# Units of 16 batches in pairs through TensorE, with K and Q products in three rotating PSUM banks

## The chip, the core and the metric

The kernel runs on one core of one Trainium2 chip. The metric is the device time of one execution in microseconds. The core has a tensor engine (PE; its weight loads are recorded apart, as PEld), a vector engine (DVE), a scalar engine (ACT), GpSimd (POOL, not used here) and SyncE (SP), whose queue issues all DMAs. PE writes only to PSUM, which has eight banks of 512 fp32 values per partition.

## The reference

```python
# F: (2048, 64, 128), W: (64, 64, 128), K_w and Q_w: (128, 128), all fp32
Kf = jnp.einsum('bjd,ed->bje', F, K_w)
S = jnp.einsum('bid,bjd->bij', F, Kf)
out = jnp.einsum('bij,ijd->bid', S, W)
out = out + jnp.einsum('bid,ed->bie', F, Q_w)
```

For each of 2048 batches: a projection of 64 tokens by K, the 64 x 64 scores of the tokens with it, then for each row i a product of the scores of all batches with W[i], and a second projection by Q that is added.

## The kernel before

The order on every engine is written out by hand, with semaphores. 2048 batches are 16 tiles (`TILES`) of 128; a tile is 8 units (`UNITS`) of 16 batches, 1024 tokens each, so that there are 128 units. In one step for unit `u` of tile `t`, PE does three blocks in this order:

- `scores(t, u)`: 16 fp32 matmuls with 64 stationary and 64 moving columns, `s_ps<-f_ring,kf`. Two batches alternate between the lower and the upper half of the output partitions. The stationary operand is `kf`, which ACT has copied out of PSUM.
- `rows_out(t - 1, u)`: 8 fp32 matmuls with a contraction over 64 partitions and 128 columns, `o_ps<-s_t,w_sb`, for four rows i of the tile before. They alternate between the lower and the upper half of the input partitions.
- `project(t, u + 1)`: 12 matmuls of 128 x 128 by 512 columns, for the next unit. Each of K and Q takes two banks, and each bank three matmuls: the fp32 product is split into `hi` and `lo` parts (`f_hi`, `f_lo`, `k_hi`, `k_lo`, `q_hi`, `q_lo`).

An fp32 matmul of the first two kinds stands as two records in the trace; so a block of scores has 32 records and a block of rows 16. The PSUM tensors `kf_ps`, `q_ps`, `s_ps` and `o_ps` have two banks each.

ACT does in each step `split_f` (`f_hi` of the unit after next), `copy_kf` (one copy of 1024 elements per partition) and `copy_q` (two of 512). DVE does `copy_s` (three copies of the scores to `s_t`), `sum_out` (`o_ps` + `q_out` to `o_sb`) and its half of the split (`f_lo`). SP issues a load of 512 KB and a store of 512 KB per unit; `o_sb` has two slots, and `sum_out` waits until the store of two units ago has landed. Tile 0 has no rows, and after the last tile 8 blocks of rows alone are left (`body(TILES, 0)`).

Of the kernel before, what the change touches and what calls it, by code (L numbers as in the profile page):

```python
# [5 lines left out]
F32 = mybir.dt.float32  # L6
# [9 lines left out]
UNITS = 8  # L16
UB = P // UNITS
# [3 lines left out]
IR = N // 2 // UNITS  # L21
HALF = N // 2
BANK = 512
RING = 4
# [3 lines left out]
def build(nc, f_t, k_t, q_t, w, out):  # L28
    with ExitStack() as ctx:
# [10 lines left out]
        f_ring = sbuf("f_ring", [D, RING, KP, 2, N])  # L40
        f_hi = sbuf("f_hi", [D, 2, TOK], F32R)
        f_lo = sbuf("f_lo", [D, 2, TOK], F32R)
        kf = sbuf("kf", [D, 2, KP, 2, N])

# [3 lines left out]
        q_out = sbuf("q_out", [D, 2, 2, HALF, P])  # L48
# [8 lines left out]
        kf_ps = psum("kf_ps", [D, 2, BANK])  # L57
        q_ps = psum("q_ps", [D, KP, 2, N])
        s_ps = psum("s_ps", [P, 2, BANK])
        o_ps = psum("o_ps", [D, 2, IR, P])  # L60

        f_in = [sem(f"f_in{n}") for n in range(RING)]
# [4 lines left out]
        qhi_done, qlo_done = sem("qhi_done"), sem("qlo_done")  # L67
        fhi_done, flo_done = sem("fhi_done"), sem("flo_done")
# [22 lines left out]
        def front(t, u):  # L91

            return not isinstance(t, int) or t * UNITS + u < FRONT

# [3 lines left out]
        def _(sp):  # L98
            def load_f(g, slot):
                sp.dma_start(f_ring[:, slot, :, :, :].rearrange("d k h i -> d (k h i)"),  # L100
                             f_t[bass.ds(g, 1), :, :].rearrange("o d n -> (o d) n")
                             ).then_inc(f_in[slot], 16)

            def load_w(half):
                rows = w.rearrange("(m s) j d -> s j m d", s=2)
                sp.dma_start(w_sb[half * N:(half + 1) * N, :, :],
                             rows[half:half + 1, :, :, :].rearrange("o j m d -> (o j) m d")
                             ).then_inc(w_in, 16)
# [8 lines left out]
            load_f(0, 0)  # L117
            sp.dma_start(k_raw[:, :], k_t).then_inc(k_in, 16)
            load_f(1, 1)
            sp.dma_start(q_raw[:, :], q_t).then_inc(q_in, 16)  # L120
            load_f(2, 2)

            def body(t, parity):
                base = t * UNITS
                for u in range(UNITS):
                    if front(t, u + 3):
                        wait(sp, s_done, base + u)
                        load_f(base + (u + 3), (u + 3) % RING)
                    if first(t) and u < 2:
                        load_w(u)  # L130
                    if not first(t):
                        if u > 0:
                            store(t - 1, u - 1, base + (u - 1 - UNITS))
                        elif not (isinstance(t, int) and t == 1):
                            store(t - 2, UNITS - 1, base - (UNITS + 1))
# [7 lines left out]
        def _(act):  # L143
            def split_f(t, u):

                g = t * UNITS + u
                act.wait_ge(f_in[u % RING], t * (UNITS // RING * 16) + (u // RING * 16 + 16))
                wait(act, q_done, g - 1)
                nc.scalar.activation(f_hi[:, u % 2, :],  # L149
                                     f_ring[:, u % RING, :, :, :].rearrange("d k h i -> d (k h i)"),  # L150
                                     COPY).then_inc(fhi_done, 1)

            def copy_kf(t, u):
                g = t * UNITS + u
# [6 lines left out]
            def copy_q(t, u, parity):  # L161
                act.wait_ge(q_done, t * UNITS + u + 1)
                if u == 0:
                    wait(act, out_done, t * UNITS - UNITS)
                src = q_ps[:, :, :, :].rearrange("d k h (m s) -> d s m h k", s=2)
                for s in range(2):
                    rows = src[:, s, :, :, :]
                    if s == 1:
                        rows = rows[:, :, ::-1, :]
# [191 lines left out]
```

## Time and profile before

| | |
|---|---|
| median of three runs | 694.48 us (694.47 to 695.4) |
| the profiled execution | 694.19 us, of which the span of the trace is 692.4 us |
| PE | 666.3 us busy, 96% of the span |
| DVE | 464.9 us, 67% |
| ACT | 393.2 us, 57% |
| q1, all loads and stores | 57.5% of 16 DMA engines, 136.46 MB |

Busy time is the union of an engine's records. A matmul's record starts when it does but its end is modelled, so that neighbours overlap; how far apart two starts are says what a matmul costs in a stream. An entry in square brackets behind a row is the idle time ahead of it and what ended it.

### The profile page before, as it was taken

What the parts mean: (1) busy time and instruction counts of PE and PEld (TensorE: products, weight loads), DVE (VectorE), ACT (ScalarE), POOL (GpSimd) and SP (SyncE); (2) the same over time, 40 slices, a digit from 0 to 9 for tenths busy, and PEclk for the clock granted to TensorE, in tenths of its full rate; (3) what the DMA queues carried; (4) which work ended last, traced back from release to release, by engine and by line L of the source; (5) the groups of instructions that cost most, each with busy time, mean ns of one, the idle gap of its engine ahead of it and who ended that gap; (6) DMA issues with size and microseconds to landing.
All of it is one profiled execution on the core that took longest, in us unless ns stands there. A gap on an engine that the chain in (4) does not pass through costs nothing.

```text
span 692.4 us, 18553 instructions
## 1 busy us (share of the span) xinstructions
PE 666.3 (96%) x7680; PEld 539.0 (78%) x7680; DVE 464.9 (67%) x642; ACT 393.2 (57%) x515; POOL 0.2 (0%) x4
## 2 busy tenths in 40 slices
PE   5999999999999999999999999999999999999953
PEld 4788887887888888878888888788788887888843
DVE  3667677676776776776767767767667677677542
ACT  5775655656656556566566565565665655655500
POOL 0000000000000000000000000000000000000000
PEclk9999999999999999999999999999999999999965
DMA  9645655565565555555555555566556555655333
GB/s 234 176 154 207 213 198 201 212 207 199 203 210 207 194 205 212 204 197 205 212 200 197 209 211 196 199 211 206 198 203 211 206 195 207 213 197 201 124 149 126
DMA packets 57694, 136.90 MB, mean 198 GB/s; under 512 B 4160, under 2 KB 8512, under 8 KB 57664
## 3 DMA queue, kind: packets, MB, share of 16 engines
q1 hardware_dynamic: 57664, 136.46, 57.5%
q8 instruction: 23, 0.38, 0.2%
q14 instruction: 7, 0.06, 0.0%
HBM read 69.34 MB, written 67.11 MB: 197 GB/s over the span
## 4 chain that ended last, share of the span: by engine, by line
PE 96%; DVE 2%; DMA 0%; issue 0%; ACT 0%; SPq 0%
PE o_ps L310 21%; PE s_ps L296 20%; PE kf_ps L272 12%; PE kf_ps L274 9%; PE q_ps L282 9%; PE kf_ps L273 9%; PE q_ps L284 9%; PE q_ps L283 8%; DVE o_sb L235 2%; DMA k_raw<-k_t 0%; DVE f_lo L202 0%; ACT f_hi L149 0%; DVE s_t L221 0%; SPq L100 0%; ACT k_hi L176 0%
## 5 line engine op out<-in xcount | busy, mean ns | idle before, releaser
L157 ACT ACTIVATE kf<-kf_ps 128x1024 f32<-128x1024 f32 x128 | 131.6, 1028 | 213.0 <-PE kf_ps L274 213.0
L218 DVE COPY s_t<-s_ps 128x256 f32<-128x256 f32 x128 | 54.4, 425 | 190.6 <-PE s_ps L296 190.6
L235 DVE TENSOR_TENSOR o_sb<-o_ps,q_out 128x1024 f32<-128x1024 f32 x128 | 156.9, 1225 | 20.6 <-PE o_ps L310 16.9
L310 PE MATMUL o_ps<-s_t,w_sb 64*128 64x128 f32 x2048 | 154.8, 293 | 11.7 <-DVE o_sb L235 11.3
L170 ACT ACTIVATE q_out<-q_ps 128x512 f32<-128x512 f32 x256 | 138.9, 595 | 46.4 <-PE q_ps L284 46.4
L296 PEld LDWEIGHTS s_ps<-f_ring,kf 128*64 128x64 f32 x4096 | 129.8, 138 | 45.1 <-ACT kf L157 44.4
L202 DVE TENSOR_TENSOR f_lo<-f_ring,f_hi 128x1024 fp32r<-128x1024 f32 x128 | 155.5, 1215 | 1.3 <-ACT f_hi L149 1.3
L296 PE MATMUL s_ps<-f_ring,kf 128*64 128x64 f32 x4096 | 147.5, 225 | 0.0
L310 PEld LDWEIGHTS o_ps<-s_t,w_sb 64*128 64x128 f32 x2048 | 129.6, 194 | 22.0 <-DVE o_sb L235 11.6
L149 ACT ACTIVATE f_hi<-f_ring 128x1024 fp32r<-128x1024 f32 x128 | 135.5, 1058 | 0.0
L272 PE MATMUL kf_ps<-f_hi,k_hi 128*128 128x512 f32 x256 | 114.9, 449 | 7.0 <-DVE f_lo L202 7.0
L274 PE MATMUL kf_ps<-f_hi,k_lo 128*128 128x512 f32 x256 | 101.6, 397 | 0.0
L282 PE MATMUL q_ps<-f_hi,q_hi 128*128 128x512 f32 x256 | 101.3, 396 | 0.0
L273 PE MATMUL kf_ps<-f_lo,k_hi 128*128 128x512 f32 x256 | 100.7, 394 | 0.0
L284 PE MATMUL q_ps<-f_hi,q_lo 128*128 128x512 f32 x256 | 100.4, 392 | 0.0
L283 PE MATMUL q_ps<-f_lo,q_hi 128*128 128x512 f32 x256 | 99.8, 390 | 0.0
L272 PEld LDWEIGHTS kf_ps<-f_hi,k_hi 128*128 128x128 f32 x256 | 48.0, 187 | 28.0 <-issue 7.0
L284 PEld LDWEIGHTS q_ps<-f_hi,q_lo 128*128 128x128 f32 x256 | 48.2, 188 | 11.7
L274 PEld LDWEIGHTS kf_ps<-f_hi,k_lo 128*128 128x128 f32 x256 | 48.3, 189 | 11.4
L283 PEld LDWEIGHTS q_ps<-f_lo,q_hi 128*128 128x128 f32 x256 | 48.3, 189 | 11.2
L282 PEld LDWEIGHTS q_ps<-f_hi,q_hi 128*128 128x128 f32 x256 | 48.3, 189 | 10.2
L224 DVE COPY s_t<-s_ps 64x256 f32<-64x256 f32 x128 | 54.6, 427 | 1.7
(11 smaller groups left out, 104.9 us busy)
## 6 DMA issues: line engine op xcount, KB each, us to landing
f_ring<-f_t SPq DMA_DIRECT2D x128, 512.0 KB, 3.3
out<-o_sb SPq DMA_DIRECT2D x128, 512.0 KB, 3.1
w_sb<-w SPq DMA_DIRECT2D x2, 1024.0 KB, 11.6
k_raw<-k_t SPq DMA_DIRECT2D x1, 64.0 KB, 3.1
q_raw<-q_t SPq DMA_DIRECT2D x1, 64.0 KB, 5.2
```

Of the source, the lines that this page charges most:

```text
L149: nc.scalar.activation(f_hi[:, u % 2, :], f_ring[:, u % RING, :, :, :].rearrange("d k h i -> d (k h i)"), COPY).then_inc(fhi_done, 1)
L170: ins = nc.scalar.activation(q_out[:, parity, s, :, u * UB:(u + 1) * UB].rearrange("d m (h k) -> d m h k", h=2), rows, COPY)
L202: nc.vector.tensor_tensor(f_lo[:, u % 2, :], f_ring[:, u % RING, :, :, :].rearrange("d k h i -> d (k h i)"), f_hi[:, u % 2, :].bitcast(F32 ...
L235: nc.vector.tensor_tensor(o_sb[:, slot, :, :], o_ps[:, :, :, :].rearrange("d s m n -> d s (m n)"), q_out[:, parity, :, u * IR:(u + 1) * IR ...
L272: nc.tensor.matmul(dst, k_hi[:, :], hi[:, cols], start=True, stop=False)
L273: nc.tensor.matmul(dst, k_hi[:, :], lo[:, cols], start=False, stop=False)
L274: ins = nc.tensor.matmul(dst, k_lo[:, :], hi[:, cols], start=False, stop=True)
L282: nc.tensor.matmul(dst, q_hi[:, :], hi[:, cols], start=True, stop=False)
L283: nc.tensor.matmul(dst, q_hi[:, :], lo[:, cols], start=False, stop=False)
L284: ins = nc.tensor.matmul(dst, q_lo[:, :], hi[:, cols], start=False, stop=True)
L296: ins = nc.tensor.matmul(s_ps[h * N:(h + 1) * N, k // (KP // 2), at:at + N], kf[:, u % 2, k, h, :], f_ring[:, u % RING, k, h, :], start=Tr ...
L310: ins = nc.tensor.matmul(o_ps[:, s, x, :], w_sb[half, m, :], s_t[half, parity, m, :], start=True, stop=True)
```

## The change

Two units go through TensorE together as a pair `p` (4 pairs a tile). PE's order in a step becomes scores of unit 2p, scores of 2p+1, rows, rows, and then the projections of the next pair. A projection is done in four chunks of 512 tokens; each chunk has one K and one Q product of one bank each, three matmuls. The eight products of a pair rotate over the three banks of `kq_ps`, so a product waits for the copy of the product three before it. ACT copies each product by itself, in 512 elements. The scores of even units now lie in a bank of `o2_ps`, which the rows of odd units also write, those of odd units in `s2_ps`, and rows of even and odd units have banks of their own (`o1_ps`, `o2_ps`).

The moving operand of half of the score matmuls and half of the row matmuls is read with its two halves swapped (`rows[:, ::-1, :]`, `cols[:, ::-1, :]`), in place of an output shifted by one element and a reversed copy of Q. Loads are of 1 MB; the first pair is loaded and split in four chunks of 256 KB, and K's weights are loaded ahead of it. ACT copies the first pair's products before it splits the second.

```diff
+        kq_ps = psum("kq_ps", [D, 3, BANK])
+        s2_ps = psum("s2_ps", [P, 1, BANK])
+        o2_ps = psum("o2_ps", [P, 2, BANK])
+        o1_ps = psum("o1_ps", [P, 2, BANK])
...
+            sp.dma_start(k_raw[:, :], k_t).then_inc(k_in, 16)
+            load_first(0)
+            load_first(1)
+            sp.dma_start(q_raw[:, :], q_t).then_inc(q_in, 16)
+            load_first(2)
+            load_first(3)
             load_f(1, 1)
-            sp.dma_start(q_raw[:, :], q_t).then_inc(q_in, 16)
             load_f(2, 2)
...
+            def copy_kf(t, p, c, bank):
+                n = (t * PAIRS + p) * CHUNKS + c
+                act.wait_ge(k_done, n + 1)
+                wait(act, s_done, (t * PAIRS + p) * 2 - 2 + c // 2 + 1)
+                nc.scalar.activation(kf[:, c // 2, c % 2 * CK:(c % 2 + 1) * CK, :, :].rearrange("d k h i -> d (k h i)"),
+                                     kq_ps[:, bank, :], COPY).then_inc(kf_copied, 1)
+
+            def copy_q(t, p, c, bank, parity):
+                n = (t * PAIRS + p) * CHUNKS + c
+                act.wait_ge(q_done, n + 1)
+                if p == 0 and c == 0:
                     wait(act, out_done, t * UNITS - UNITS)
...
+                at = (2 * p + c // 2) * KP + c % 2 * CK
+                nc.scalar.activation(
+                    q_out[:, parity, :, :].rearrange("d i (h b) -> d i h b", h=2)[:, :, :, at:at + CK],
+                    kq_ps[:, bank, :].rearrange("d (k h i) -> d i h k", k=CK, h=2), COPY).then_inc(q_copied, 1)
+
+            def copy_pair(t, p, parity):
+                for c in range(CHUNKS):
+                    copy_kf(t, p, c, 2 * c % 3)
+                    copy_q(t, p, c, (2 * c + 1) % 3, parity)
...
+                    if c == 0:
+                        wait(pe, kf_copied, n)
+                    elif c >= 2:
+                        pe.wait_ge(q_copied, n - 1)
+                    three(kq_ps[:, 2 * c % 3, :], k_hi, k_lo, hi, lo).then_inc(k_done, 1)
...
+                        pe.wait_ge(kf_copied, n)
+                    three(kq_ps[:, (2 * c + 1) % 3, :], q_hi, q_lo, hi, lo).then_inc(q_done, 1)
...
+                        rows = f_ring[:, p % RING, e, k, h, :].rearrange("d (s m) -> d s m", s=2)
+                        if h:
+                            rows = rows[:, ::-1, :]
...
+                if e and not (isinstance(t, int) and t == TILES - 1):
+                    pe.wait_ge(s_copied, h + UNITS)
+                wait(pe, out_done, h - 1)
...
             def body(t, parity):
-                for u in range(UNITS):
-                    if front(t, u):
-                        scores(t, u)
+                for p in range(PAIRS):
+                    if front(t, p):
+                        scores(t, p, 0)
+                        scores(t, p, 1)
                     if not first(t):
-                        rows_out(t - 1, u, 1 - parity)
-                    if front(t, u + 1):
-                        project(t, u + 1)
+                        rows_out(t - 1, p, 0, 1 - parity)
+                        rows_out(t - 1, p, 1, 1 - parity)
+                    if front(t, p + 1):
+                        project(t, p + 1)
```

On PE, in the body of the loop over tiles, one step before reads as follows (the name is the output tensor and its inputs, "waits" the semaphores):

```order
L296 MATMUL s_ps<-f_ring,kf 64x64 [waits s_copied,kf_copied]
L296 MATMUL s_ps<-f_ring,kf 64x64 x15
L76 REGISTER_ALU
L310 MATMUL o_ps<-s_t,w_sb 128x128 [waits out_done]
L310 MATMUL o_ps<-s_t,w_sb 128x128 x7
L267 REGISTER_ALU
L272 MATMUL kf_ps<-f_hi,k_hi 128x512 [waits kf_copied,flo_done]
```

In the changed kernel the same place reads so, with the first two products of the projections that follow:

```order
L340 MATMUL s2_ps<-f_ring,kf 64x64 x15
L359 MATMUL o1_ps<-s_t,w_sb 128x128 [waits out_done]
L359 MATMUL o1_ps<-s_t,w_sb 128x128 x7
L359 MATMUL o2_ps<-s_t,w_sb 128x128 [waits out_done,s_copied]
L359 MATMUL o2_ps<-s_t,w_sb 128x128 x7
L296 MATMUL kq_ps<-f_hi,k_hi 128x512 [waits kf_copied,flo_done]
L297 MATMUL kq_ps<-f_lo,k_hi 128x512
L298 MATMUL kq_ps<-f_hi,k_lo 128x512
L296 MATMUL kq_ps<-f_hi,q_hi 128x512 [waits q_copied]
```

Two blocks of each kind now stand together, each still with a wait at its head, and each product of three matmuls is a group with a wait of its own.

On ACT one step before is five copies, of which only the first three wait:

```order
L149 ACTIVATE f_hi<-f_ring 128x1024 [waits q_done,f_in3]
L155 REGISTER_ALU
L157 ACTIVATE kf<-kf_ps 128x1024 [waits s_done,k_done]
L170 ACTIVATE q_out<-q_ps 128x32x16 [waits q_done]
L170 ACTIVATE q_out<-q_ps 128x32x16
```

In the changed kernel, for a pair, two splits stand ahead of eight copies that alternate between K and Q:

```order
L175 ACTIVATE f_hi<-f_ring 128x1024 [waits q_done]
L175 ACTIVATE f_hi<-f_ring 128x1024
L181 ISA
L84 ISA [waits k_done]
L183 ACTIVATE kf<-kq_ps 128x512 [waits s_done]
L84 ISA [waits q_done]
L192 ACTIVATE q_out<-kq_ps 128x128x4 [waits out_done]
L181 REGISTER_ALU
L183 ACTIVATE kf<-kq_ps 128x512 [waits s_done,k_done]
L192 ACTIVATE q_out<-kq_ps 128x128x4 [waits q_done]
```

Each of the eight copies waits for PE, and PE waits for each of them three products later.

## Rows read from the trace of the kernel before

**Rows 1.** The page: busy time, and the chain that ended last.

```profile
PE 666.3 (96%) x7680; PEld 539.0 (78%) x7680; DVE 464.9 (67%) x642; ACT 393.2 (57%) x515; POOL 0.2 (0%) x4
PE 96%; DVE 2%; DMA 0%; issue 0%; ACT 0%; SPq 0%
```

**Rows 2.** Windows of one step: length, then each engine's busy time, clock, DMA.

```profile
300.99:302.07 1.08, 1.08 (x33) 1.01 (x33) 0.00 (x0) 0.97 (x3) 0.00 (x0) 1.00 0.99 375
302.07:303.16 1.09, 1.09 (x20) 0.97 (x16) 0.94 (x3) 1.05 (x2) 0.00 (x0) 1.00 0.27 100
303.16:306.13 2.97, 2.97 (x15) 2.17 (x13) 2.68 (x3) 1.03 (x1) 0.00 (x0) 1.00 0.51 180
```

**Rows 3.** Timeline of PE, narrow windows of that step: start, duration, line, how many.

```profile
301.68 0.46 PE L296 MATMUL s_ps<-f_ring,kf 128*64 128x64 f32 x10
301.85 0.29 PE L296 MATMUL s_ps<-f_ring,kf 128*64 128x64 f32 x4
302.73 0.50 PE L310 MATMUL o_ps<-s_t,w_sb 64*128 64x128 f32 x6
302.84 0.39 PE L310 MATMUL o_ps<-s_t,w_sb 64*128 64x128 f32 x4
303.16 0.50 PE L272 MATMUL kf_ps<-f_hi,k_hi 128*128 128x512 f32 x1
303.50 0.40 PE L273 MATMUL kf_ps<-f_lo,k_hi 128*128 128x512 f32 x1
...
304.43 0.39 PE L274 MATMUL kf_ps<-f_hi,k_lo 128*128 128x512 f32 x1
304.66 0.40 PE L282 MATMUL q_ps<-f_hi,q_hi 128*128 128x512 f32 x1
305.81 0.39 PE L284 MATMUL q_ps<-f_hi,q_lo 128*128 128x512 f32 x1
306.13 1.15 PE L296 MATMUL s_ps<-f_ring,kf 128*64 128x64 f32 x32
```

**Rows 4.** Timeline of ACT, DVE and SP, the same step.

```profile
302.19 0.42 DVE L218 COPY s_t<-s_ps 128x256 f32<-128x256 f32 x1 [1.46 <-PE s_ps L296]
303.51 1.23 DVE L235 TENSOR_TENSOR o_sb<-o_ps,q_out 128x1024 f32<-128x1024 f32 x1
304.86 1.03 ACT L157 ACTIVATE kf<-kf_ps 128x1024 f32<-128x1024 f32 x1 [1.73 <-PE kf_ps L274]
304.90 0.56 SPq L113 DMA_DIRECT2D out<-o_sb  x1
306.24 1.08 ACT L170 ACTIVATE q_out<-q_ps 128x512 f32<-128x512 f32 x2 [0.35 <-PE q_ps L284]
```

**Rows 5.** Groups of instructions: busy us, mean ns of one, idle before.

```profile
L170 ACT ACTIVATE q_out<-q_ps 128x512 f32<-128x512 f32 x256 | 138.9, 595 | 46.4 <-PE q_ps L284 46.4
L149 ACT ACTIVATE f_hi<-f_ring 128x1024 fp32r<-128x1024 f32 x128 | 135.5, 1058 | 0.0
L202 DVE TENSOR_TENSOR f_lo<-f_ring,f_hi 128x1024 fp32r<-128x1024 f32 x128 | 155.5, 1215 | 1.3 <-ACT f_hi L149 1.3
L218 DVE COPY s_t<-s_ps 128x256 f32<-128x256 f32 x128 | 54.4, 425 | 190.6 <-PE s_ps L296 190.6
L242 DVE TENSOR_TENSOR k_lo<-k_raw,k_hi 128x128 fp32r<-128x128 f32 x1 | 0.3, 293 | 4.7 <-ACT k_hi L176 4.7
```

**Rows 6.** Timeline of the beginning.

```profile
1.18 0.41 SPq L118 DMA_DIRECT2D k_raw<-k_t  x1
4.34 0.31 ACT L176 ACTIVATE k_hi<-k_raw 128x128 fp32r<-128x128 f32 x1 [2.33 <-DMA k_raw<-k_t]
7.01 0.77 PE L272 MATMUL kf_ps<-f_hi,k_hi 128*128 128x512 f32 x1 [7.01 <-DVE f_lo L202]
10.98 0.40 PE L282 MATMUL q_ps<-f_hi,q_hi 128*128 128x512 f32 x1
11.77 1.15 PE L296 MATMUL s_ps<-f_ring,kf 128*64 128x64 f32 x32
15.80 1.15 PE L296 MATMUL s_ps<-f_ring,kf 128*64 128x64 f32 x32
```

**Rows 7.** Timeline of the end, and a window of it.

```profile
656.11 1.15 PE L296 MATMUL s_ps<-f_ring,kf 128*64 128x64 f32 x32
661.21 1.23 DVE L235 TENSOR_TENSOR o_sb<-o_ps,q_out 128x1024 f32<-128x1024 f32 x1 [1.35 <-PE o_ps L310]
685.07 1.23 DVE L235 TENSOR_TENSOR o_sb<-o_ps,q_out 128x1024 f32<-128x1024 f32 x1 [2.18 <-PE o_ps L310]
...
672.00:693.00 21.00, 8.32 (x64) 7.14 (x64) 5.57 (x5) 0.00 (x0) 0.00 (x0) 0.50 0.34 127
```

**Rows 8.** DMA issues: size and median us from issue to landing.

```profile
out<-o_sb SPq DMA_DIRECT2D x128, 512.0 KB, 3.1
```

More of the change, by code:

```diff
@@ L46, in build @@
         w_sb = sbuf("w_sb", [P, HALF, D])
-        q_out = sbuf("q_out", [D, 2, 2, HALF, P])
+        q_out = sbuf("q_out", [D, 2, N, P])
         o_sb = sbuf("o_sb", [D, OBUF, 2, IR * P])
@@ new lines, in split_f @@
+            def split_f(t, p):
+                slot = p % RING
+                act.wait_ge(f_in[slot], t * 16 + (p // RING * 16 + (16 if slot else 0)))
+                wait(act, q_done, (t * PAIRS + p) * CHUNKS - CHUNKS)
+                for e in range(2):
+                    nc.scalar.activation(f_hi[:, p % 2 * 2 + e, :],
+                                         f_ring[:, slot, e, :, :, :].rearrange("d k h i -> d (k h i)"),
+                                         COPY).then_inc(fhi_done, 1)
@@ L287, in scores, with three, project @@
-            def scores(t, u):
-                g = t * UNITS + u
-                pe.wait_ge(kf_copied, g + 1)
-                wait(pe, s_copied, g)
+            def three(dst, w_hi, w_lo, hi, lo):
+                nc.tensor.matmul(dst, w_hi[:, :], hi, start=True, stop=False)
+                nc.tensor.matmul(dst, w_hi[:, :], lo, start=False, stop=False)
+                return nc.tensor.matmul(dst, w_lo[:, :], hi, start=False, stop=True)
+            def project(t, p):
+                v = t * PAIRS + p
+                begin = isinstance(v, int) and v == 0
+                for c in range(CHUNKS):
+                    n = v * CHUNKS + c
+                    unit = p % 2 * 2 + c // 2
+                    cols = slice(c % 2 * BANK, (c % 2 + 1) * BANK)
+                    hi, lo = f_hi[:, unit, cols], f_lo[:, unit, cols]
+                    if begin:
+                        pe.wait_ge(flo_first, c + 1)
+                    elif c % 2 == 0:
+                        pe.wait_ge(flo_done, v * 2 - 2 + c // 2 + 1)
+                    if c == 0:
[3 more added lines that the diff above has]
+                    three(kq_ps[:, 2 * c % 3, :], k_hi, k_lo, hi, lo).then_inc(k_done, 1)
+                    if begin and c == 0:
+                        pe.wait_ge(qlo_done, 1)
+                    if c == 0:
+                        wait(pe, q_copied, n)
+                    else:
+                        pe.wait_ge(kf_copied, n)
+                    three(kq_ps[:, (2 * c + 1) % 3, :], q_hi, q_lo, hi, lo).then_inc(q_done, 1)
@@ L353 @@
     r = run_bass_kernel_spmd(nc, [arrays], core_ids=[0])
[L355 to L360 removed]
+    o = np.asarray(r.results[0]["out"]).reshape(TILES, D, N, 2, N)
+    return np.ascontiguousarray(o.transpose(0, 4, 3, 2, 1)).reshape(B, N, D)
```

243 lines of the change are left out of this document (106 added, 137 removed).

## The prediction

> **What bounds the kernel now.** I read the page first: PE is busy for 96% of the span and the chain that ended last is PE's for 96% [rows 1]. So almost nothing can be won from another engine, except at the two ends; what counts is how PE's time is made up. The windows of one step show it: 1.08 us for the block of scores, 1.09 for the rows, 2.97 for the projections, 5.14 together, with PE busy throughout and its clock at 1.00, the 2.4 GHz level [rows 2]. A busy PE is not a streaming PE, so I went on to the starts in narrow windows [rows 3]:
>
> - Scores: from 301.68 (10 records left) to 301.85 (4 left) are three matmuls of two records each, 0.17 us: 0.058 each by finer division (the block's first 11 took 0.69, of which the first about 0.11).
> - Rows: 302.73 (6 left) to 302.84 (4 left), one matmul: 0.112.
> - Projections: 304.43 to 304.66 is 0.23.
>
> In a stream the step would be 16 x 0.058 + 8 x 0.112 + 12 x 0.23 = 0.93 + 0.90 + 2.76 = 4.59 us. It takes 5.14. The missing 0.55 lies at the three borders between blocks, each in two pieces [rows 3]. Scores to rows: the last score matmul starts at 301.91 and the next block at 302.07, 0.16 where 0.058 is usual (+0.10), and the first row matmul holds the second up by another 0.10 (302.07 to 302.73 are five matmuls, 0.66 in place of 0.56). Rows to projections: 302.95 to 303.16 where 0.112 is usual (+0.10), then 303.16 to 303.50 where 0.23 is usual (+0.11). Projections to scores: 305.81 to 306.13 where 0.23 is usual (+0.09), and about 0.05 at the first score matmul. Sum 0.545.
>
> The list of waits blames ACT's copy of `kf` for the last of these. I don't believe it: that copy runs from 304.86 to 305.89 [rows 4], and scores start at 306.13, 0.24 later; the sum at 303.51 [rows 4] and other releases follow their release by about 0.05. The border costs what the other two cost, and there nobody is late.
>
> **The steady part.** Per pair the change keeps 32 score, 16 row and 24 projection matmuls, and has three borders between kinds in place of six. If blocks of one kind adjoin at stream rate, a pair takes 2 x 5.14 - 0.545 = 9.74 us in place of 10.28. That adjoining blocks of one kind are free although each has a wait at its head is not shown for scores or rows; the nearest row is the border from K to Q, which has a satisfied wait on `q_copied` and costs the usual 0.23 (304.43 to 304.66, rows 3 show it). I take nothing for it, and as the other end the full price of a border, 0.18.
>
> The Trainium skill ("TensorEngine Tiling (Array Packing)", Key Properties) states that changing the tiling mode, as against the tile, drains TensorE. The three kinds of block here are three modes (128*64, 64*128, 128*128 in the rows), and by that rule adjoining blocks of one kind would cost nothing; by the reading that a wait costs it, the sum below would be 22.7 us higher. The trace agrees with it at the border from K to Q, 0.23 us.
>
> Tiles 1 to 15 have 60 pairs, and 59 periods from the first to the last: 59 x 0.545 = 32.2 us.
>
> Does anyone else now hold PE up? **ACT's copies** are the new risk. A K product's third matmul starts at 304.43 and ACT's copy at 304.86 [rows 3, 4]: 0.43 later. A copy of 512 elements out of PSUM takes 0.595 [rows 5], two back to back 1.08 [rows 4]. With three banks, product n+3 may start when copy n is done: third matmul of n at X, copy done at X + 0.43 + 0.60 + 0.05 = X + 1.08; product n+3 starts at X + 0.23 + 2 x 0.69 = X + 1.61, its weights load 0.23 earlier, X + 1.38. Slack 0.3. In rate, a product takes PE 3 x 0.23 = 0.69 and ACT 0.60 even without overlap. So no stall, as long as a copy takes less than 0.69. The Q copy now writes runs of four elements where it wrote runs of eight, twice; an operation with runs of eight shows no price for them: DVE's copy of scores has 256 elements in 425 ns, and a contiguous subtraction 128 in 293 and 1024 in 1215, which is 161 + 1.03 a column and gives 425 for 256 [rows 5]. I take 0; above, I leave room for 0.03 a copy beyond 0.69, 0.24 us a pair. The work of splitting goes after the last copy: two of 1.06 [rows 5] while PE does scores and rows, 4.1 us.
>
> **DVE**: three score copies are 1.32 us (302.19 to 303.51 [rows 4]), a sum 1.25, a split 1.22. For a pair 7.6 of 9.74. The tightest new wait is that of the rows of the odd unit for the scores copy of the even one (shared bank): the scores of the even unit end 1.0 after the pair's start, DVE begins some 0.15 later (302.07 to 302.19), the copy ends at 2.5, the odd rows start at 3.1. Slack about 0.6. The sum of the odd unit ends at 6.4, the next pair's scores need it at 9.74.
>
> **The swapped moving operands** (16 + 8 matmuls of a pair): no row shows a matmul with such an operand. Runs are 32 and 64 elements. I take nothing (the strided copies above show none); as the other end 2 ns a record, the fixed part that separates 29 ns a record from 64 columns at 2.4 GHz (26.7): 48 x 2 = 0.1 us a pair, 6 us. The Trainium skill ("SBUF — State Buffer", cachelines) asks for two or more hits on a 16-byte line, which runs of 32 elements, and runs of four in `q_out`, satisfy; no run here shows it.
>
> **The beginning.** K's weights are issued first, at 0.73 in place of 1.18, with 3.15 to the first use [rows 6]; 3.9. The first chunk follows at about 4.3, its split in halves 0.60 (ACT) and 161 + 512 x 1.03 = 0.69 (DVE): PE starts at 5.65 in place of 7.01 [rows 6]. The first nine matmuls take 3.97 us, until 10.98 [rows 6], 0.44 each, about half speed; I keep that. Then 15 x 0.23: the products of pair 0 end at 13.1, its scores at 15.1. Here something new is late: ACT splits pair 1 only after pair 0's last copy (13.9), hi at 14.95, lo 1.22 later: PE resumes at 16.3, 1.1 late, and once more 0.3 because the split of pair 2 stands before the copies of pair 1. The pairs of tile 0 have no rows: 2 x 4.03 (11.77 to 15.80 [rows 6]) - 0.34 = 7.7. Fourth projection (tile 1) starts at 16.3 + 0.35 + 3 x 7.7 = 39.75, its scores at 45.45. Before, the scores of the same unit start at 11.77 + 8 x 4.03 = 44.0, but without the 2.76 of a second unit's projections. Gain 44.0 + 2.76 - 45.45 = 1.3.
>
> **The end.** Before, PE and DVE take turns on one `o_ps`, 3.4 us a unit, PE's clock at 0.50, the 1.2 GHz level, from about 662 on [rows 7]. With two sets of banks PE does the next rows during the sum. What comes next is the store: `sum_out` of unit h needs the landing of unit h-2: 1.23 + 0.16 to the issue (304.74 to 304.90 [rows 4]) + 3.1 [rows 8] + 0.05 = 4.55 per two units. Even at the low clock a block of rows is 2.1 and hides. 512 KB per 2.3 us is 230 GB/s, below the 375 seen [rows 2]. Counted from the start of the last pair's scores: its sums end at 5.15 and 6.4, then even sums at 9.7, 14.25, 18.8, 23.35 and odd ones to 24.6. Before, from unit 126's scores at 656.11 - 5.14 = 650.97 to the last sum's end at 686.30 [rows 7] are 35.3, of which 2.97 are projections that now lie ahead: 32.4. Gain 7.8.
>
> **Sum.** 32.2 + 1.3 + 7.8 = 41.3. The span of 692.4 becomes 651.1. The profiled execution was 694.19 with its span 692.4, 1.8 outside: 652.9; the median of the runs is 0.3 above that execution: **653.2 us**.
>
> **The rivals.**
>
> - *A border is paid at a wait, not at a change of shape.* For it: each border between kinds has a wait. Against: K to Q. Adjoining blocks of scores and rows then cost 0.18 each, 0.36 a pair, over 63 pairs 22.7: 676. Chance 0.09.
> - *ACT's copies become the pace in the projections.* Eight copies of c us: the pair grows by 8(c - 0.69). At 0.72, 0.24 x 62 = 15: 668. Chance 0.07. This is also the rival on the other side: the 41 us are eaten when 8(c - 0.69) = 0.66, c = 0.775; the kernel is slower if a copy with its handshake takes longer than that, 0.18 above the 0.595 of rows 5. For c = 0.80, 0.88 x 62 = 54.6: 708. Chance 0.05.
> - *Swapped operands cost*, 2 ns a record: 659; chance 0.07, inside the range.
> - *The borders stay, the change helps only the ends* (no gain in the steady part): 685; chance 0.03. No change within 0.2% would need such a mixture by accident: 0.02.
>
> The likeliest, with 0.67, has its own range: 647 to 658, from the beginning (2 up or down), the copy's first stalls and the landing of stores in the tail (3.0 to 3.4, eight units). The range for 8 in 10 takes in the dearer operands and copies at 0.72: 646 to 670. About 0.2% is what a measurement of this kernel tells from no change. Faster 0.93 (0.67 + 0.09 + 0.07 + 0.07 + 0.03), same 0.02, slower 0.05.
>
> **What would show it.** In the steady part a period of 9.74 from one even block of scores to the next; inside, 64 records of scores with starts at a steady 0.058, no break in the middle. Each K to Q start in `kq_ps` 0.23 after the one before: a larger figure there is ACT. In the tail DVE's idle time ended by the store's DMA and no longer by PE. Wrong would be: a break at adjoining blocks, ACT copies over 0.69, or starts of score matmuls more than 0.058 apart.

## The result, and the profile after

The changed kernel takes 701.91 us (median of four runs, 699.71 to 702.22) beside 694.49 of the kernel before on the same chip. The ratio is 1.0096 [1.0082, 1.011]: slower by 1.0%, where 653.2 us and faster by 6% had been forecast. The profiled execution has a span of 700.2 us.

The page of the changed kernel: busy time, the tenths in which PE was busy and its clock, the instruction queue, and the chain that ended last.

```profile
PE 641.9 (92%) x7680; PEld 542.1 (77%) x7680; DVE 463.4 (66%) x644; ACT 426.5 (61%) x645; POOL 0.2 (0%) x4
PE   5999999996999969999699996999969999999974
PEclk9999999998999999999899997999989999999995
q8 instruction: 68, 1.11, 0.6%
PE 44%; DMA 34%; DVE 10%; issue 7%; SPq 2%; ACT 2%; DVEq 0%; ACTq 0%
```

PE is busy for 24 us less than before [rows 1], as it should be, but the span is 8 us longer: PE now stands still. The row of tenths shows where. Five 6s, evenly spaced, stand among the 9s, and the clock row dips below four of them. They are five slices of 17.5 us apart, one turn of the loop over tiles.

The timeline of PE in the changed kernel, first a pair in the middle of a turn, then the place of the first dip:

```profile
308.08 0.39 PE L298 MATMUL kq_ps<-f_hi,q_lo 128*128 128x512 f32 x1
308.39 1.15 PE L340 MATMUL o_ps<-f_ring,kf 128*64 128x64 f32 x32
309.38 1.10 PE L340 MATMUL s_ps<-f_ring,kf 128*64 128x64 f32 x32
310.41 2.06 PE L359 MATMUL o_ps<-s_t,w_sb 64*128 64x128 f32 x32
312.39 0.50 PE L296 MATMUL kq_ps<-f_hi,k_hi 128*128 128x512 f32 x1
...
163.73 0.39 PE L298 MATMUL kq_ps<-f_hi,q_lo 128*128 128x512 f32 x1
169.69 0.59 PE L340 MATMUL o_ps<-f_ring,kf 128*64 128x64 f32 x6 [5.57 <-issue]
```

The pair at 308.39 is what had been predicted. Its second block of scores follows the first without a break, 0.99 us later, the 16 row matmuls run as one stream, and the next pair's scores start at 318.08, a period of 9.69 us where 9.74 was forecast. At 163.73 PE starts the last matmul of a turn and at 169.69 the first one of the next, 5.96 us later. PE is idle for 5.57 of them, and the entry says "issue": no semaphore that the trace shows ended it.

Lines from the list of waits of the changed kernel (us in total, times, longest):

```profile
PEld o_ps L340 <- issue: 51.5, 64, 6.8
DVE o_sb L263 <- DMA out<-o_sb: 35.1, 41, 3.0
PE o_ps L340 <- issue: 28.6, 5, 6.4
ACT q_out L192 <- DVE o_sb L263: 14.3, 12, 1.7
PE kq_ps L296 <- ACT q_out L192: 8.2, 12, 1.1
```

"28.6, 5" are the five places. Starts of the matmuls on both sides are 5.96, 6.14, 5.43, 6.75 and 6.25 us apart, each at the back edge of the loop (the jump from the end of the loop's code to its start). Windows around the first (length, then PE, PEld, DVE, ACT and POOL busy, granted clock, DMA share, GB/s):

```profile
163.00:164.00 1.00, 1.00 (x5) 0.57 (x4) 0.00 (x0) 0.90 (x2) 0.00 (x0) 1.00 0.72 238
...
165.00:166.00 1.00, 0.00 (x0) 0.00 (x0) 0.00 (x0) 1.00 (x2) 0.00 (x0) 1.00 0.93 361
...
167.00:168.00 1.00, 0.00 (x0) 0.00 (x0) 0.00 (x0) 0.00 (x0) 0.00 (x0) 1.00 0.00 0
168.00:169.00 1.00, 0.00 (x0) 0.00 (x0) 0.00 (x0) 0.00 (x0) 0.00 (x0) 0.60 0.00 0
...
172.00:173.00 1.00, 1.00 (x24) 1.00 (x23) 0.97 (x3) 0.00 (x0) 0.00 (x0) 0.50 0.00 0
...
174.00:175.00 1.00, 1.00 (x14) 1.00 (x14) 0.69 (x2) 0.00 (x0) 0.00 (x0) 0.50 0.00 0
175.00:176.00 1.00, 1.00 (x20) 0.97 (x18) 0.48 (x1) 0.00 (x0) 0.00 (x0) 0.99 0.00 0
```

After some four idle microseconds the granted clock goes to 0.50, the 1.2 GHz level, and comes back near 175. So the stop is paid twice: the pair runs its scores and rows at half speed.

**Where the time went.** Periods between starts of a pair's first scores, against 9.69 of an undisturbed pair, from the trace after:

| 59 periods of tiles 1 to 15 | periods, us | over 9.69 each, us |
|---|---|---|
| 5 that hold a back edge | 16.36, 16.55, 15.85, 16.71, 16.11 | 33.1 |
| 5 behind them | 12.06, 11.01, 12.16, 12.32, 11.34 | 10.4 |
| 9 other ends of a tile, and one more | 9.97 to 11.09 | 8.4 |
| 39 others | 9.69 | 0 |

46.1 (scores of tile 1 start) + 59 x 9.69 + 51.9 + 30.5 (from the last pair's scores at 669.65 to the end at 700.2) = 700.2. The first two excesses, 43.5 us, lie at the back edges, but not all of it is the stop. Against the usual 0.32 from the last product to the next scores, the five stops take 28.9 us; the slow pairs behind them take 10.4; and inside the same five periods PE waits for a PSUM bank, 0.40 to 0.96 us each and 3.7 together, as it does at other ends of a tile (see the account of the steps below).

What happens there? The page's q8 row is the queue that brings instructions. The kernel before had 23 packets in all, 0.38 MB, and none while PE was in its loop (148.5 to 577.5). After, there are 68 of 16 KB, one about every 10 us all through, nine for each turn. The packets in two stretches of the changed kernel, 163 to 166.8 and 166.8 to 168 (packets, MB, share of the DMA engines):

```profile
q1 hardware_dynamic: 361, 1.14, 81.4%
...
q8 instruction: 1, 0.02, 5.0%
q1 hardware_dynamic: 2, 0.00, 0.2%
```

While PE stands, 1.14 MB of data pass, then at 166.87 one packet of code, then PE goes on. The Trainium skill ("Runtime: NRT & Kernel Launch", Instruction fetch mechanics) says that PE's instruction memory holds 128 KiB or 2048 instructions, that it is filled in blocks of 16 KiB (256 instructions), and that a taken branch whose target is outside the current window of two pages forces a fetch before execution goes on. The trace agrees on the blocks (1.11 MB in 68 packets) and not on the window: the kernel before jumps back over eight blocks in each turn and fetches nothing. A turn of PE's loop was 1983 instructions before and is 2034 after (the new groups of three matmuls bring waits and register arithmetic of their own); the records between two branches in the traces give the same counts.

The branch itself has a record, on PE's instruction stream (first in the kernel before, then in the changed one; shortest, median and longest duration in ns of the six, the last of which leaves the loop and is not taken):

```profile
L328 PEldq COMPARE_BRANCH  x6: 80/220/262, 164.0 to 575.2; - x6
L379 PEldq COMPARE_BRANCH  x6: 87/6474/7145, 162.8 to 599.3; - x6
```

A taken branch took 0.22 to 0.26 us before and 5.8 to 7.1 after.

### The profile page after: what moved, and what is told of

The parts are those of the page before. It is cut to its first block, busy times and chain, and to the rows that moved or that the text cites. A ratio compares the mean times of both kernels' runs of the same rounds, so it can differ in the third digit from the quotient of the medians.

```text
span 700.2 us, 19021 instructions
## 1 busy us (share of the span) xinstructions
PE 641.9 (92%) x7680; PEld 542.1 (77%) x7680; DVE 463.4 (66%) x644; ACT 426.5 (61%) x645; POOL 0.2 (0%) x4
## 3 DMA queue, kind: packets, MB, share of 16 engines
q8 instruction: 68, 1.11, 0.6%
## 4 chain that ended last, share of the span: by engine, by line
PE 44%; DMA 34%; DVE 10%; issue 7%; SPq 2%; ACT 2%; DVEq 0%; ACTq 0%
DMA out<-o_sb 33%; PE kq_ps L296 10%; PE kq_ps L298 8%; PE kq_ps L297 8%; DVE o_sb L263 8%; PE o_ps L359 7%; PE o_ps L340 6%; PE s_ps L340 4%; SPq L129 1%; ACT q_out L192 1%; DVE s_t L252 1%; DVE s_t L253 1%; DVE s_t L251 1%; SPq L114 1%; DMA f_ring<-f_t 1%
## 5 line engine op out<-in xcount | busy, mean ns | idle before, releaser
L183 ACT ACTIVATE kf<-kq_ps 128x512 f32<-128x512 f32 x256 | 153.2, 599 | 202.1 <-PE kq_ps L298 186.1
L263 DVE TENSOR_TENSOR o_sb<-o_ps,q_out 128x1024 f32<-128x1024 f32 x128 | 154.8, 1223 | 39.9 <-DMA out<-o_sb 35.1
L192 ACT ACTIVATE q_out<-kq_ps 128x512 f32<-128x512 f32 x256 | 153.2, 599 | 33.0 <-DVE o_sb L263 14.3
L296 PE MATMUL kq_ps<-f_hi,k_hi 128*128 128x512 f32 x256 | 108.7, 424 | 15.8 <-ACT q_out L192 8.2
L340 PE MATMUL o_ps<-f_ring,kf 128*64 128x64 f32 x2048 | 77.8, 232 | 28.6 <-issue 28.6
L296 PE MATMUL kq_ps<-f_hi,q_hi 128*128 128x512 f32 x256 | 100.9, 394 | 0.3 <-ACT kf L183 0.3
L298 PE MATMUL kq_ps<-f_hi,k_lo 128*128 128x512 f32 x256 | 101.0, 395 | 0.0
L297 PE MATMUL kq_ps<-f_lo,k_hi 128*128 128x512 f32 x256 | 100.5, 393 | 0.0
L298 PE MATMUL kq_ps<-f_hi,q_lo 128*128 128x512 f32 x256 | 100.0, 391 | 0.0
L297 PE MATMUL kq_ps<-f_lo,q_hi 128*128 128x512 f32 x256 | 99.9, 390 | 0.0
L340 PE MATMUL s_ps<-f_ring,kf 128*64 128x64 f32 x2048 | 74.5, 229 | 0.0
```

The lines of the kernel that those rows point to most:

```text
L183: nc.scalar.activation(kf[:, c // 2, c % 2 * CK:(c % 2 + 1) * CK, :, :].rearrange("d k h i -> d (k h i)"), kq_ps[:, bank, :], COPY).then_i ...
L192: nc.scalar.activation(q_out[:, parity, :, :].rearrange("d i (h b) -> d i h b", h=2)[:, :, :, at:at + CK], kq_ps[:, bank, :].rearrange("d ...
L263: nc.vector.tensor_tensor(o_sb[:, slot, :, :], o_banks(e)[:, :, :], q_out[:, parity, :, :].rearrange("d (s m) b -> d s (m b)", s=2)[:, :, ...
L296: nc.tensor.matmul(dst, w_hi[:, :], hi, start=True, stop=False)
L297: nc.tensor.matmul(dst, w_hi[:, :], lo, start=False, stop=False)
L298: return nc.tensor.matmul(dst, w_lo[:, :], hi, start=False, stop=True)
```

## The experiments

Ratios are to the kernel before, timed on the same chip. Theory A said: the loop's code is too long to stay. Its rivals: the stop is a matter of some engine's wait at the back edge (B), of the new waits themselves (C), or of the kind of instructions in the loop (E).

**1. No loop.** The change as it is, written out.

```diff
-            with nc.Fori(1, TILES // 2 - 1, engines=[pe.engine], hint_back_edge=True) as pair:
-                body(pair * 2, 0)
-                body(pair * 2 + 1, 1)
+            for t in range(TILES + 1):
+                body(t, t % 2)
```

> The changed kernel with the loop over tiles written out on every engine, so that no branch is taken. Theory A (at the loop's end PE's code of the loop's start is no longer there and must be fetched, 5.4 to 6.8 us each time, five times, and the next pair runs at the 1.2 GHz level): all five gaps go and the 10 us of slow pairs behind them, together 33 + 10 = 43 of the 700.2 us span; about 659 us. Theory B (the gaps are a wait for data at every second tile's start, such as a late 1 MB load): the gaps stay where they are, about 702 us. In both, the stops of about 1 us in other tiles' last pair stay.

656.02 us, 0.9436 [0.939, 0.9483]. The place where the back edge was, in the timeline of PE:

```profile
164.08 0.39 PE L292 MATMUL kq_ps<-f_hi,q_lo 128*128 128x512 f32 x1
164.40 1.15 PE L334 MATMUL o_ps<-f_ring,kf 128*64 128x64 f32 x32
```

The next scores start 0.32 after the last product. The code is still fetched all along, 61 packets, but in order, and no stop shows. The whole loss is the loop's, and without it the change is worth 38 us of the 41 forecast (35 against the control of run 10, which has no loop either).

**2. A shorter loop.** Inside the loop PE drops the waits that other waits imply; 1989 instructions a turn.

```diff
...
-                wait(pe, s_copied, g - 1)
+                if isinstance(t, int):
+                    wait(pe, s_copied, g - 1)
...
-                wait(pe, out_done, h - 1)
+                if isinstance(t, int):
+                    wait(pe, out_done, h - 1)
```

> The changed kernel, its loop kept, without those waits of PE inside the loop that another wait already implies; 45 instructions fewer per turn, 1989 in place of 2034 (the kernel before: 1983). No work and no dependency changes. Theory A with a limit on size (the body of before still fits into what PE keeps, that of after doesn't): as the unrolled one, about 659 us, and instruction transfers stop during the loop. Theory B, or a branch that costs whatever the size: about 702 us. Theory C (the waits' own dispatch is what costs): the gain is spread over all pairs, their 9.69 us falls, the gaps stay.

661.08 us, 0.9507 [0.9461, 0.9552]. The page has `q8 instruction: 23`, no packet between 149.2 and 557.1, and the loop's tile-end pairs take 9.83 to 9.85 but for the first, 10.85. The other pairs still take 9.69, which speaks against C. One stop remains, where the loop is left for the code behind it: PE is idle for 4.8 us there, and the pair takes 16.08, 6.4 more than usual.

**3. The kernel before, with a longer loop.** Waits that are long satisfied, in `project` inside the loop: 2015 and 2047 instructions a turn. Three waits in one place make one more instruction in the trace, since the others ride on it and on the matmul behind it. The diff is that of the 2047.

```diff
+                    if not isinstance(t, int) and b in (0, 1):
+                        for _ in range(3):
+                            pe.wait_ge(w_in, 32)
...
```

> The same with 32 more: 2015 per turn, between before (1983) and after (2034). It brackets the size: with theory A either about 735 us (limit below 2015) or 694.5 us (limit between 2015 and 2034). Theories B and C: 694.5 to 695.5 us.

> The kernel before with 64 more instructions in PE's loop, waits that are long satisfied (51 ns each in a slot of 230 ns), spread over the projections: 2047 per turn. Theory A: five gaps of 5 to 7 us at the loop's end and a slow start behind each, and instruction transfers all through the loop; 694.5 + 5 x 8 = about 735 us. Theory B and C: no gap, 694.5 to 696 us.

695.05 us, 0.9998 [0.9979, 1.0016], and 695.54, 1.0001 [0.9982, 1.002], both with 23 packets and no stop. 2047 instructions stay and 2034 of the changed kernel don't: length alone isn't it. If memory is held in blocks of 256, what counts is how many blocks the loop touches, and that depends on where it begins. That is theory D: eight blocks stay, nine don't.

**4. The changed kernel's loop moved, its body untouched.** 232 more instructions that are satisfied waits, ahead of the loop (2n + 1 waits in one place make n instructions).

```diff
...
+                    for _ in range(2 * n + 1):
+                        pe.wait_ge(khi_done, 1)
...
```

> The changed kernel with 232 more instructions on PE ahead of the loop (satisfied waits in tiles 0 and 1, at most two in a slot of 230 ns), the loop itself untouched: 2034 instructions a turn. Theory D (code is kept in blocks of 16 KB, 256 instructions, which are the packets of the instruction queue; the loop stays if the blocks that it touches are eight, not nine): from the runs so far, with 1725 instructions ahead of it a loop of 2047 stays, with 1753 ahead one of 1989 stays and one of 2034 doesn't; all three hold if the loop of before starts within an instruction or two of a block's start, and then 1985 ahead puts the changed loop 4 behind one. Its gaps vanish, as in the lean kernel: about 661 us. Theory E (the register and fused instructions of the changed loop, 84 where the padded kernels have 28, are at fault): 702 us. Theory A (a count between 1989 and 2034): 702 us.

660.72 us, 0.9499 [0.9442, 0.9556]. The stops are gone and the instruction queue is idle in the loop, with the same 2034 instructions a turn:

```profile
q8 instruction: 24, 0.39, 0.2%
DVE o_sb L263 <- DMA out<-o_sb: 13.9, 14, 3.1
PE o_ps L351 <- issue: 5.3, 1, 5.3
```

The one stop of 5.3 lies where the loop is left, as in run 2. 232 instructions that do nothing take 41 us away. This is the plainest proof of D, and ends theory E on the kind of instructions.

**5. The cure undone by a shift.** The shorter loop of run 2 with 100 waits ahead of it.

> The lean kernel (1989 instructions a turn, 661.1 us) with 100 more on PE ahead of the loop. Theory D: the loop now starts 128 behind a block's start, 128 + 1989 is over 2048, nine blocks, and the gaps come back: about 700 us. Theories A and E: 661 to 662 us.

692.23 us, 0.9956 [0.9933, 0.9979]; 69 packets, back-edge pairs of 14.33 to 14.76 and 11.1 to 12.2 behind them. Again D, with shorter stops (4.8 to 5.2 us between starts) than the 700 us had reckoned with.

**6. The unchanged kernel shifted by 100, its loop untouched; and padded to 2111 a turn.**

> The kernel before with 100 more instructions on PE ahead of the loop (satisfied waits), its loop of 1983 untouched. By theory D it now starts some 100 behind a block's start and touches nine blocks, so that code is fetched all through the loop. What is open is when that costs a stop: the kernel before with 2111 a turn fetched all along and had none. D1 (a stop only where the loop's entry lies inside a block, since the next block in order is then wanted before the target's rest is there): gaps of 4 to 6 us at five back edges and slow pairs behind them, about 725 us. D2 (the stop is peculiar to the changed kernel, its larger loads or its denser PE): fetching, no gap, 694 to 696 us.

> The kernel before with 128 more instructions in PE's loop (satisfied waits, two in a slot of 230 ns): 2111 a turn, over eight blocks wherever it starts. Theories A and D: gaps of 5 to 7 us at each back edge, 694.5 + 5 x 8 = about 735 us. Theory E: 695 us.

The shifted one: 706.59 us, 1.0179 [1.0159, 1.02], 69 packets, five stops. The kernel before gets slower than the changed one by nothing but 100 idle instructions ahead of its loop. It lies between its two theories: the stops are there, as D1 had them, but shorter than forecast (2.43, 2.37, 1.69, 2.05, 2.15 between starts), and PE's clock stays at 1.00 behind four of them. Behind the second it is at 0.50 for some 3 us:

```profile
169.74 0.98 PE L308 MATMUL s_ps<-f_ring,kf 128*64 128x64 f32 x26 [2.05 <-issue]
...
170.00:171.00 1.00, 1.00 (x33) 0.93 (x30) 0.00 (x0) 0.00 (x0) 0.00 (x0) 1.00 0.06 16
...
254.00:255.00 1.00, 0.99 (x19) 1.00 (x21) 0.00 (x0) 0.17 (x1) 0.00 (x0) 0.50 0.06 16
```

The profiled span is 11.4 us longer than before (703.8 beside 692.4). The five steps with a stop account for 9.1, the step at the lower clock for 1.5, the stretch behind the last scores for 1.1 and the beginning for 0.3, less 0.5 that the kernel before loses in one late step.

The padded one: 694.36, 0.9978 [0.9948, 1.0007], 69 packets and no stop of the matmuls at all, a miss for D's price. The records of the branch show why (first the shifted kernel, then the padded one):

```profile
L340 PEldq COMPARE_BRANCH  x6: 87/4796/5130, 164.2 to 586.0; - x6
L334 PEldq COMPARE_BRANCH  x6: 88/1608/1660, 164.8 to 576.0; - x6
```

PE's instruction stream stands still in the padded kernel too, for 1.6 us at each back edge. But in the kernel before and its variants the branch is reached 2.4 to 3.1 us ahead of the start of the turn's last matmul: the matmuls in front of it have been handed over already and run on. Where the branch ends before they do, nothing is seen. In the changed kernel this lead is only 0.9, so that nearly all of the branch's time is a stop of PE. The likely reason is that each product of three now has a wait of its own, at which the instruction stream is held; no run tests it.

**7. Does a loop that begins with a block escape?** One theory was that only an entry inside a block stops PE: 229 ahead of the loop, so that it starts 1 behind a block's start, and 2098 instructions a turn, so that nine are touched.

> The changed kernel with 229 more instructions ahead of the loop, so that it starts 1 behind a block's start, and 64 more inside it (satisfied waits), 2098 a turn: nine blocks. D1: code is fetched all through, no gaps, about 661 us. D2: gaps as in the changed kernel, about 702 us.

702.12 us, 1.0115 [1.0095, 1.0135], stops of 4.86 to 5.99 us: it fell.

**8. What sets the length of a stop.** SP issues each pair's 1 MB load earlier, so that it has landed when PE comes to the back edge. With it the store of each odd unit moves from behind the load to ahead of it. PE's program is untouched.

```diff
-                    if front(t, p + 3):
-                        wait(sp, s_done, t * UNITS + 2 * p)
-                        load_f(t * PAIRS + (p + 3), (p + 3) % RING)
+                    if not first(t):
+                        if p:
+                            store(t - 1, 2 * p - 1, t * UNITS + (2 * p - 1 - UNITS))
...
+                    if front(t, p + 4):
+                        sp.wait_ge(s_done, t * UNITS + (2 * p + 2))
+                        load_f(t * PAIRS + (p + 4), p % RING)
...
+                        store(t - 1, 2 * p, t * UNITS + (2 * p - UNITS))
```

> The changed kernel, where SP issues the load of 1 MB of a pair four pairs ahead right behind the pair's own scores (some 2.2 us into a period) in place of three pairs ahead at some 4.7 us, so that it has landed before the back edge at 9.7. PE's program and its place in memory are unchanged, so its code is still fetched anew in each turn. Theory Q (the packet of code stands in the DMA queues behind the data of the load in flight: in the changed kernel the branch is at some 164.1, the packet starts at 166.86, PE resumes at 169.69): the stops at the five back edges shrink from 5.4 to 6.7 us to some 2.5 to 3.5, and the time falls by 10 to 18 us, to 684 to 692, with perhaps 3 to 5 more from stores that land sooner. Theory N (the stop is what fetching costs wherever the branch falls, data or not): stops of 5 to 7 us as before, 697 to 702.

672.65 us, 0.968 [0.9661, 0.97], with the code still fetched in every turn. Its page, its waits, its timeline and the window in which the packet passes:

```profile
q8 instruction: 68, 1.11, 0.7%
PE o_ps L342 <- issue: 14.0, 5, 3.0
163.70 0.39 PE L300 MATMUL kq_ps<-f_hi,q_lo 128*128 128x512 f32 x1
166.76 1.98 PE L342 MATMUL o_ps<-f_ring,kf 128*64 128x64 f32 x32 [2.68 <-issue]
DMA packets 1, 0.02 MB, mean 14 GB/s; under 512 B 0, under 2 KB 0, under 8 KB 0
```

In the stretch 163.8 to 165 the only packet of any queue is that of code. The stops shrink to 3.06 to 3.38 us between starts, as theory Q had it. The time fell by more than expected, 29 us (the span by 26.2; the profiled execution is the slowest of the five): periods with a back edge are 12.65 to 12.97 (17.7 less in all), those behind them lose 2.6 less, and the other tile ends 6.3 less. At these `sum_out` waits less for stores (35.1 us of such waits became 10.5); whether because the load is out of the way or because half of the stores are issued ahead of it, the run doesn't separate. Packets, branches and stops read together, the first back edge of each kernel in the trace:

| | branch starts | it takes | last matmul of the turn | packet of code starts | PE resumes | packet to PE |
|---|---|---|---|---|---|---|
| changed kernel | 162.84 | 6.38 | 163.73 | 166.87 | 169.69 | 2.82 |
| its load earlier | 162.83 | 3.47 | 163.70 | 163.95 | 166.76 | 2.81 |
| before, shifted by 100 | 164.23 | 5.13 | 167.30 | 166.99 | 169.74 | 2.74 |
| run 7 | 163.24 | 5.89 | 164.01 | 166.71 | 169.59 | 2.88 |
| run 5 | 161.26 | 5.41 | 162.13 | 164.26 | 166.94 | 2.68 |
| before, padded to 2111 | 164.77 | 1.64 | 167.18 | 163.95 | 167.50 | no stop |

In all 25 stops at back edges of the five kernels that have them PE resumes 2.60 to 3.19 us after the packet starts, mostly 2.8. The branch itself ends 2.3 to 2.7 us after the packet starts, and it does so at the five back edges of the padded kernel as well. What differs is when the packet starts. It starts behind the load in flight where there is one: at this back edge 4.0 us after the branch in the changed kernel, 2.8 in the shifted kernel before with its loads of 512 KB, 1.1 with the load moved. (The expectation put the branch at 164.1; its record is at 162.84.) In the padded kernel it starts 0.8 to 0.9 us ahead of the branch. Why that one asks for its packet so much earlier no run tells; what the trace adds is that its branch still takes 1.6 us, which the matmuls handed over before cover.

**9. Versions that gather the gains,** four slots of `o_sb` in place of two, with run 2's loop and with none.

```diff
-OBUF = 2
+OBUF = 4
```

> The lean kernel with four slots of o_sb in place of two, so that a sum no longer waits for the store of two units ago. In the loop the fourth pair's 0.15 us go (12 x 0.15 = 2); in the tail the sums no longer take 4.5 us per two units but 2 x 1.38 (512 KB at 375 GB/s) to 2 x 2.1 (rows at the 1.2 GHz level): 2 to 7 us less. Together 652 to 657 us. If stores were not what the tail waits for: 661 us.

> The unrolled form of the changed kernel with four slots of o_sb: the best version that the runs point to. Unrolling took the lean kernel's 661.1 to 656.0 (no stop where the loop is left), four slots took it to 651.3; if the two add, 646 us. If code fetches of a straight program stand in for what the slots gave: 650 to 652.

651.28 us, 0.9367 [0.9323, 0.9411], a little less than expected, and 647.93, 0.9336 [0.932, 0.9351], the fastest, between the two expectations. DVE's wait for stores goes from 15.3 to 1.5 us or less:

```profile
DVE o_sb L257 <- DMA out<-o_sb: 1.5, 1, 1.5
PE o_ps L353 <- DVE o_sb L257: 3.4, 5, 1.6
```

**10. The control:** the kernel before without its loop.

> A control: the kernel before with its loop written out. Its loop has no gap at a back edge, so that unrolling can give only the 0.46 us where the loop is left: 693.5 to 695 us by every theory. If it were faster by more, unrolling would have a merit of its own and would have to be taken off the changed kernel's gain.

690.9 us, 0.9951 [0.9932, 0.9971], a span of 689.1 beside 692.4, more of a gain than expected. The loop as such cost the kernel before 3.3 us, of which 2.6 lie behind the last sum: the last sum starts at 684.37 and ends at 685.6, 3.5 before the end, where it was 6.1 [rows 7]. Against this control the written-out change is at 0.9436 / 0.9951 = 0.948 (worked out from the two ratios).

## Why the prediction was wrong, by its own steps

**The step that failed** is "Does anyone else now hold PE up?". It went through ACT and DVE, whose semaphores PE waits for, and not through the supply of PE's own instructions. The time that PE's code takes to arrive is in no term of the sum. The change takes no matmul away and adds waits to the groups of three, 51 instructions a turn; its loop, which had touched eight blocks of 256, touched nine. The stops at the back edges cost 28.9 us and the slow pairs behind them 10.4, together 39.3. With 12.1 of waits at ends of a tile (below) they swallow the forecast gain of 41.3. By the move of the loop in run 4 the fetching is worth 41.2 us of the span, 700.2 to 659.0, although a stop where the loop is left comes in. None of the rivals named it: the one on the slower side, ACT's copies as the pace, gave 708 for another reason and did not occur. The count of blocks can be made from programs alone: with one unknown offset for all kernels, the loop before begins with a block (0 + 1983 in 2048), the padded one just fits (0 + 2047), the changed one, with 1753 instructions ahead of its loop where there were 1725, begins 28 in (28 + 2034 = 2062 does not), and the shifts give 4 + 2034 (fits), 28 + 1989 (fits), 128 + 1989, 100 + 1983, 0 + 2111 and 1 + 2098 (none fits). That puts all these loops, and the one of 2015, on the right side. The offset is fitted to them, so it is a reading and not a separate proof; the moves by 232 and 100 are the proof.

**Borders between blocks: right.** 9.69 measured, 9.74 forecast; 59 x (10.28 - 9.69) = 34.8 in place of 32.2. Adjoining blocks of one kind cost nothing though each has a wait at its head: from the last start of one block to the first of the next the median is 58 ns for scores and 112 for rows, as inside a block. So the border is paid at a change of kind, not at a wait. The rule of the Trainium skill that the prediction weighed ("TensorEngine Tiling (Array Packing)", Key Properties) agrees with the trace at 308.39 to 312.39, where no border of 0.18 shows between two blocks of scores or of rows. A pair in a stream would take 32 x 0.058 + 16 x 0.112 + 24 x 0.23 = 9.17 us, which leaves 0.52 for its three borders, where 0.545 was taken.

**ACT's copies: right on rate.** 599 ns each, for Q as for K, where 595 was taken, and K to Q stays 0.23 in mid-tile. The group of the page after:

```profile
L183 ACT ACTIVATE kf<-kq_ps 128x512 f32<-128x512 f32 x256 | 153.2, 599 | 202.1 <-PE kq_ps L298 186.1
L192 ACT ACTIVATE q_out<-kq_ps 128x512 f32<-128x512 f32 x256 | 153.2, 599 | 33.0 <-DVE o_sb L263 14.3
```

**Swapped operands: free.** In each block plain and swapped matmuls take turns, so the starts tell them apart: the median from one start to the next over tiles 1 to 15 is 58 ns behind a plain and behind a swapped score matmul, and 112 and 112 ns in the rows. The rival with 2 ns a record would have given 62 and 116.

**Overlooked: the wait at a tile's end.** This one, too, belongs to "Does anyone else now hold PE up?". The first `copy_q` of tile t waits for the last sum of tile t - 2, which comes only in the same step, as in the kernel before; but now K and Q share three banks, so that PE waits for `copy_q` three products later, and the sum waits for a store. The chain in the timeline of the changed kernel:

```profile
159.12 1.23 DVE L263 TENSOR_TENSOR o_sb<-o_ps,q_out 128x1024 f32<-128x1024 f32 x1 [0.71 <-DMA out<-o_sb]
160.38 0.60 ACT L192 ACTIVATE q_out<-kq_ps 128x512 f32<-128x512 f32 x1 [1.36 <-PE kq_ps L298]
161.12 0.47 PE L296 MATMUL kq_ps<-f_hi,k_hi 128*128 128x512 f32 x1 [0.75 <-ACT q_out L192]
```

The sum begins 0.71 late for its store and ends at 160.35, the copy starts at 160.38 (the entry names PE, whose product was long done; the sum is what came last), and PE gets its bank at 161.12 where 160.21 was due, 0.23 after the start at 159.98. It comes to 8.4 us over the tile ends outside the back edges and 3.7 inside the back-edge periods. It is not independent of the fetching: in run 4, with the same loads, stores and slots, the ends of a tile inside the loop but for the first take 9.90 to 9.92, 0.2 over the usual. In run 8, with the stores landing sooner, the 8.4 are 2.1. So most of the 12.1 came with the stops; how the two hang together is not shown.

**The beginning: 0.65 too early.** PE starts at 6.58 where 5.65 was forecast. K's weights were there at 2.62, ahead of the 3.9 forecast, but the first chunks of F landed late:

```profile
2.62 0.31 ACT L202 ACTIVATE k_hi<-k_raw 128x128 fp32r<-128x128 f32 x1 [0.61 <-DMA k_raw<-k_t]
5.08 1.27 ACT L165 ACTIVATE f_hi<-f_ring 128x512 fp32r<-128x512 f32 x2 [2.15 <-DMA f_ring<-f_t]
6.58 0.76 PE L296 MATMUL kq_ps<-f_hi,k_hi 128*128 128x512 f32 x1 [6.58 <-DVE f_lo L229]
```

Tile 1's scores start at 46.1, forecast 45.45.

**The end: right as a sum, by luck: two errors cancel.** From the last pair's scores to the last sum's end 27.0 us instead of 24.6. The sums wait for the stores, as forecast, and of the last ten stores seven take 3.05 to 3.2 us to land, near the 3.1 of rows 8; but the first two take 4.0 and 4.1 and the fourth 5.0. Behind the last sum 3.5 instead of 6.1, a difference that the control of run 10 shows without the change too. Together 30.5, forecast 30.7:

```profile
695.43 1.23 DVE L263 TENSOR_TENSOR o_sb<-o_ps,q_out 128x1024 f32<-128x1024 f32 x1 [2.00 <-DMA out<-o_sb]
```

**The sum, corrected:** forecast span 651.1, + 51.9 (28.9 stops, 10.4 slow pairs, 12.1 tile ends, 0.5 not assigned), - 59 x 0.05 = 3.0 (border), + 0.65 (beginning), - 0.2 (end) = 700.4, measured 700.2.
